# First expert's first layer for all 128 tokens, ahead of the routing result, with the tokens picked afterwards by the placement matrix

## The reference, cut to what matters

```python
x = x + gnn(layernorm(x), edge_index, W1, ..., W2, ...)          # x: (128, 768)
z = layernorm(x)
probs = softmax(z @ Wg + bg)                                      # Wg: (768, 8)
top_p = max(probs); comb = one_hot(argmax(probs)) * top_p
h = gelu(einsum('bnd,edh->ebnh', z, W1) + b1)                     # W1: (8, 768, 3072)
y = einsum('ebnh,ehd->ebnd', h, W2) + b2                          # W2: (8, 3072, 768)
ffn_out = einsum('ebnd,bne->bnd', y, comb)
scores = sigmoid(z @ Wm + bm)                                     # threshold: 12th largest score
x = x + ffn_out + small correction from ffn_out @ Wv, scores and Wo
```

## Time and profile before

| what | value |
|---|---|
| median of 3 runs | 503.6 us (502.79 to 503.71) |
| the profiled execution | 506.07 us, of which the span of the trace is 504.3 us |
| TensorE busy, matmuls | 466.4 us (92%), 2310 instructions |
| VectorE, ScalarE, GpSimd busy | 137.0, 60.6 and 33.9 us |
| read from HBM | 189.62 MB, mean 377 GB/s |
| end of the graph phase (`used` = 32) | about 151.7 us |
| first `up(0)` of the first expert | 164.85 us |
| end of the first expert's round | about 202.5 us |

### The profile page before, as it was taken

How to read it: one execution, slowest core, us unless ns; L and a number is a source line. 1 busy time by engine, 2 the same in 40 slices (tenths; PEclk the granted TensorE clock), 3 DMA queues, 4 the chain that set the end, 5 groups by cost and what they waited for, 6 DMA issues and landing times.

```text
span 504.3 us, 6062 instructions
## 1 busy us (share of the span) xinstructions
PE 466.4 (92%) x2310; PEld 232.4 (46%) x2310; DVE 137.0 (27%) x362; ACT 60.6 (12%) x113; POOL 33.9 (7%) x52
## 2 busy tenths in 40 slices
PE   7999998999999999999999999998898889789892
PEld 5656665667558344344344353352243224224352
DVE  6573698426206311010010010020010002001165
ACT  1110212002003020021020020110020011002100
POOL 3262240000000000210000000000000000000000
PEclk9999999999999999999999999999999999999996
DMA  8889998898999999999999999999999999999700
GB/s 309 305 301 402 401 400 297 307 407 323 411 357 369 417 425 423 414 423 423 423 429 423 422 428 427 420 423 430 423 423 426 427 422 423 427 423 424 297 1 31
DMA packets 32541, 190.22 MB, mean 377 GB/s; under 512 B 5423, under 2 KB 5631, under 8 KB 18190
## 3 DMA queue, kind: packets, MB, share of 16 engines
q1 hardware_dynamic: 31694, 189.94, 92.6%
q0 software_dynamic: 544, 0.05, 0.1%
q10 hardware_dynamic: 288, 0.03, 0.0%
HBM read 189.62 MB, written 0.39 MB: 377 GB/s over the span
## 4 chain that ended last, share of the span: by engine, by line
PE 60%; SPq 16%; DMA 15%; DVE 5%; issue 2%; ACT 1%; POOL 0%; DVEq 0%
PE ps L1286 17%; PE ps L1259 16%; PE ps L1081 11%; SPq L337 8%; DMA chunk<-in_L_ffn_W 7%; DMA lower<-in_L_ffn_W 6%; PE ps L1041 6%; SPq L316 4%; SPq L332 3%; PE ps L1272 2%; PE ps L1069 2%; DMA slot<-in_L_gnn_W 2%; PE ps L1096 2%; PE ps L1221 2%; SPq L354 1%
## 5 line engine op out<-in xcount | busy, mean ns | idle before, releaser
L1286 PE MATMUL ps<-lower,hidden 128*64 128x384 f32 x600 | 102.9, 491 | 6.1 <-DMA lower<-in_L_ffn_W 6.1
L1259 PE MATMUL ps<-chunk,gathered 128*64 128x512 f32 x408 | 92.6, 597 | 10.0 <-DMA chunk<-in_L_ffn_W 10.0
L1286 PEld LDWEIGHTS ps<-lower,hidden 128*64 128x64 f32 x600 | 41.3, 136 | 58.3 <-issue 45.1
L1041 PE MATMUL ps<-slot,xT 128*128 128x384 f32 x192 | 64.1, 488 | 1.2 <-DMA slot<-in_L_gnn_W 1.2
L1259 PEld LDWEIGHTS ps<-chunk,gathered 128*64 128x64 f32 x408 | 27.5, 136 | 66.9 <-issue 47.6
L1081 PE MATMUL ps<-slot,eluT 128*128 128x384 f32 x168 | 55.3, 486 | 0.0
L866 DVE TENSOR_TENSOR biased<-ps,b_T 128x384 f32<-128x384 f32 x32 | 17.1, 554 | 133.5 <-PE ps L1272 133.5
L1041 PEld LDWEIGHTS ps<-slot,xT 128*128 128x128 f32 x192 | 35.6, 190 | 23.9 <-issue 1.3
L1259 PE MATMUL ps<-extra,gathered 128*64 128x512 f32 x168 | 38.9, 598 | 4.7 <-DMA extra<-in_L_ffn_W 4.6
L1081 PEld LDWEIGHTS ps<-slot,eluT 128*128 128x128 f32 x168 | 31.5, 190 | 20.7
L874 DVE TENSOR_SCALAR place_top<-slot_no,rank,small 128x128 f32<-128x128 f32 x8 | 2.8, 346 | 136.7 <-PE ps L1309 136.7
(11 more groups left out here) (288 smaller groups left out, 282.2 us busy)
## 6 DMA issues: line engine op xcount, KB each, us to landing
lower<-in_L_ffn_W SPq DMA_DIRECT2D x50, 1152.0 KB, 26.1
chunk<-in_L_ffn_W SPq DMA_DIRECT2D x34, 1536.0 KB, 22.7
slot<-in_L_gnn_W SPq DMA_DIRECT2D x31, 1152.0 KB, 12.7
extra<-in_L_ffn_W SPq DMA_DIRECT2D x14, 1536.0 KB, 27.7
lower_on<-in_L_ffn_W SPq DMA_DIRECT2D x14, 1152.0 KB, 30.9
slot<-in_L_gnn_W SPq DMA_DIRECT2D x3, 384.0 KB, 4.6
x_sb<-in_x SPq DMA_DIRECT2D x1, 384.0 KB, 3.4
out<-xc SPq DMA_DIRECT2D x1, 384.0 KB, 2.3
```

The source lines that it names most:

```text
L1041: last = T.matmul(ps[:, 2 * (h % 2) + b, 0:HB], xT[:, 3 * half + k, :], slots[n % RING][:, k, b * HB:(b + 1) * HB], start=(n % 2 == 0 and ...
L1259: last = T.matmul(ps[b * CAP:(b + 1) * CAP, s, 0:BANK], gathered[:, k, :], upper_homes[k][:, at:at + BANK], start=(k == 0), stop=(k == KT ...
L1286: last = T.matmul(ps[c * CAP:(c + 1) * CAP, 4, 0:HB], hidden[:, q, k, b, :], lower_homes[i][:, k, c * HB:(c + 1) * HB], start=(i == 0 and ...
```

## The change

The first expert's first layer no longer waits for the gate. It is computed for all 128 tokens. What VectorE and ScalarE copy out of PSUM lands in chunk 5's own memory, scaled by the reciprocal of the standard deviation, and `first_turn` multiplies that by `place_now`: one product both picks the expert's tokens and turns the result. The gate, the ranks and the scores stand between the six `first_up`. The mean is taken out of `x1` itself, ahead of its transposes; it comes from a one-column matmul over row sums. The initial gather, the centring of the gate's weights and the `stay_warm` groups 5 to 8 are gone. SyncE's program is the same; the sixth count of `used` in the first round now comes from the first matmul of `down(0)`. The diff, cut to its core:

```diff
@@ ScalarE
-            S.copy(blocks(h2_sb[:, :]), ps[:, 0:2, 0:HB]).then_inc(h2_ready, 1)
+            S.activation(blocks(h2_sb[:, :]), ps[:, 0:2, 0:HB], ACT.Identity, accum_out=col(HSUM)).then_inc(h2_ready, 1)
...
+            act.wait_ge(mean2_ready, 1)
+            S.activation(x1[:, HB:D], x1[:, HB:D], ACT.Identity, bias=col(MEAN)).then_inc(base_half, 1)
             act.wait_ge(xT_done, 3)
-            S.copy(xT[:, 0:3, :].rearrange("p k t -> p (k t)"), ps[:, 5, 0:HB]).then_inc(xT_first, 1)
-            act.wait_ge(mean2_ready, 1)
-            S.activation(xc[:, :], x1[:, :], ACT.Square, bias=col(MEAN), accum_out=col(SS)).then_inc(squares, 1)
+            S.copy(xT[:, 0, :], ps[:, 5, 0:P]).then_inc(xT_first, 1)
+            act.wait_ge(xT_done, 4)
+            S.copy(xT[:, 1:3, :].rearrange("p k t -> p (k t)"), ps[:, 7, P:HB]).then_inc(xT_second, 1)
+            act.wait_ge(x1_part, 3)
+            S.activation(xc[:, :], x1[:, :], ACT.Square, accum_out=col(SS)).then_inc(squares, 1)
...
+                if first:
+                    for s in range(3):
+                        act.wait_ge(up_done, s + 1)
+                        S.activation(chunks[CHUNKS - 1][:, s * BANK:(s + 1) * BANK], ps[:, s, 0:BANK], ACT.Identity,
+                                     scale=col(RSTD)).then_inc(upper_ready, 1)
+                    gelu(0)
+                    gelu(1)
+                    turn_place()
+                    gelu(2)
+                    gelu(3)
+                    return
@@ VectorE
-            centre_gate()
             dve.wait_ge(att_ready, 3)
-            for b in range(2):
-                dve.wait_ge(out2_done, b + 1)
-                V.scalar_tensor_tensor(out=x1[:, b * HB:(b + 1) * HB], in0=ps[:, 2 + b, 0:HB], scalar=col(RS),
-                                       in1=x1[:, b * HB:(b + 1) * HB], op0=ALU.mult, op1=ALU.add,
-                                       accum_out=sums2[:, b:b + 1]).then_inc(x1_half, 1)
...
+            step(V.tensor_scalar(col(SHARE), col(RS), -1.0 / D, None, ALU.mult))
+            dve.wait_ge(out2_sum, 1)
+            dve.wait_ge(base_ready, 1)
+            V.tensor_scalar(col(MEAN), ps[:, 7, 0:1], col(SHARE), col(BASE), ALU.mult,
+                            ALU.add).then_inc(mean2_ready, 1)
             dve.wait_ge(mean2_ready, 1)
+            step(V.tensor_scalar(x1[:, 0:HB], x1[:, 0:HB], col(MEAN), None, ALU.add))
+            for first, end in ((0, P), (P, HB), (HB, D)):
+                half = first // HB
+                dve.wait_ge(out2_done, half + 1)
+                if half:
+                    dve.wait_ge(base_half, 1)
+                V.scalar_tensor_tensor(out=x1[:, first:end], in0=ps[:, 2 + half, first - HB * half:end - HB * half],
+                                       scalar=col(RS), in1=x1[:, first:end], op0=ALU.mult,
+                                       op1=ALU.add).then_inc(x1_part, 1)
...
-            for half in range(2):
-                dve.wait_ge(gather_done if half else gather_half, 1)
...
+                if first:
+                    for s in range(3):
+                        dve.wait_ge(wide_done, s + 1)
+                        V.tensor_scalar(chunks[CHUNKS - 1][:, WIDE + s * BANK:WIDE + (s + 1) * BANK],
+                                        ps[:, 3 + s, 0:BANK], col(RSTD), None, ALU.mult).then_inc(wide_ready, 1)
+                    add_bias(0)
+                    add_bias(1)
+                    dve.wait_ge(turned, QU)
+                    next_place()
+                    add_bias(2)
+                    take_gathered(1, 5)
+                    take_threshold()
+                    add_bias(3)
+                    return
@@ TensorE
+            T.matmul(ps[:, 7, 0:1], att_T[:, 0, :], col(HSUM), start=True, stop=True).then_inc(out2_sum, 1)
...
+            def first_up(k):
+
+                pe.wait_ge(lead_in[k], 16)
+                for bank in (0, 3, 1, 4, 2, 5):
+                    last = T.matmul(ps[:, bank, 0:BANK], xT[:, k, :], chunks[k][:, bank * BANK:(bank + 1) * BANK],
+                                    start=(k == 0), stop=(k == KT - 1))
+                    if k == KT - 1:
+                        last.then_inc(up_done if bank < 3 else wide_done, 1)
+                if k < KT - 1:
+                    last.then_inc(used, 1)
+
+            def first_turn(q):
+
+                pe.wait_ge(upper_ready, min(q + 1, 3))
+                pe.wait_ge(wide_ready, min(q + 1, 3))
                 for k in range(3):
-                    c = (3 * half + k) * P
-                    last = T.matmul(ps[:, 3 if half else 5, k * CAP:(k + 1) * CAP], xn[:, c:c + P],
-                                    place_now[:, :], start=True, stop=True)
-                last.then_inc(gather_done if half else gather_half, 1)
-            pe.wait_ge(score_ready, 1)
-            T.matmul(ps[0:1, 4, 0:P], col(SCORE), ident[:, :], start=True, stop=True).then_inc(score_turned, 1)
+                    for b in range(2):
+                        c = b * WIDE + q * HB
+                        last = T.matmul(ps[:, q, k * P + b * CAP:k * P + (b + 1) * CAP],
+                                        chunks[CHUNKS - 1][:, c + k:c + HB:3], place_now[:, :], start=True, stop=True)
+                last.then_inc(turned, 1)
...
+                                if first and i == 0 and k == 0 and c == 0:
+                                    last.then_inc(used, 1)
```

More of the change, by code:

```diff
@@ L1184, in _ @@
                      stop=True).then_inc(att_scores, 1)
[L1185 to L1188, removed]
             stay_warm(WARM[3])
@@ L1196, in _ @@
                          start=True, stop=True).then_inc(out2_done, 1)
[L1197 to L1214, removed]
-            T.matmul(ps[:, 6, 0:EXPERTS], ones[:, :], hot, start=True, stop=True).then_inc(rank_done, 1)
-            stay_warm(WARM[8], 0)
+            pe.wait_ge(mean2_ready, 1)
+            for i, (first, end, bank, at) in enumerate(((0, P, 5, 0), (P, HB, 7, P), (HB, D, 6, 0))):
+                pe.wait_ge(x1_part, i + 1)
+                for c in range(first, end, P):
+                    last = T.transpose(ps[:, bank, at + c - first:at + c - first + P], x1[:, c:c + P], ident[:, :])
+                last.then_inc(xT_done, 1)
             def gather(bank):
@@ L1243, in round_ @@
             def round_(r, first=False):
-                upper_homes, lower_homes = (chunks, lowers) if first else (chunks_on, lowers_on)
+                lower_homes = lowers if first else lowers_on
                 def landed(i):
@@ L1288, in down @@
                                                 start=(i == 0 and k == 0), stop=(i == DOWN - 1 and k == 2))
+                                if first and i == 0 and k == 0 and c == 0:
+                                    last.then_inc(used, 1)
                         last.then_inc(used, 1)
                 if first:
[L1292 to L1301 removed]
+                    pe.wait_ge(xT_first, 3)
@@ new lines, in round_ @@
+                    first_up(0)
+                    pe.wait_ge(xT_second, 1)
+                    pe.wait_ge(xT_third, 1)
+                    for k in range(KT):
+                        last = T.matmul(ps[:, 7, 0:EXPERTS + 1], xT[:, k, :], gate_w[:, k, :], start=(k == 0),
+                                        stop=(k == KT - 1))
+                    last.then_inc(logit_done, 1)
+                    first_up(1)
+                    pe.wait_ge(onehot_ready, 1)
+                    T.matmul(ps[:, 7, 16:24], later[:, :], hot, start=True, stop=True).then_inc(rank_done, 1)
@@ new lines, in round_ @@
+                    T.matmul(ps[:, 6, 0:EXPERTS], ones[:, :], hot, start=True, stop=True).then_inc(rank_done, 1)
+                    first_up(2)
+                    pe.wait_ge(score_ready, 1)
+                    T.matmul(ps[0:1, 7, P:2 * P], col(SCORE), ident[:, :], start=True,
+                             stop=True).then_inc(score_turned, 1)
+                    pe.wait_ge(top_ready, 1)
+                    T.matmul(ps[0:EXPERTS, 6, 0:P], hot_top[:, :], ident[:, :], start=True,
+                             stop=True).then_inc(hot_turned, 1)
@@ new lines, in round_ @@
+                    first_up(3)
+                    pe.wait_ge(thr_ready, 1)
+                    first_ffn()
+                    first_up(4)
+                    first_up(5)
+                    pe.wait_ge(place_ready, 1)
+                    for q in range(QU):
+                        first_turn(q)
+                    T.transpose(ps[:, 5, HB:512], place_top[:, :], ident[:, :]).then_inc(place_turned, 1)
+                    down(0)
+                    down(1)
+                    T.matmul(ps[:, 3, HB:HB + 1], ones[0:1, :], top16[0:1, KEEP - 1:KEEP], start=True,
+                             stop=True).then_inc(thr_done, 1)
@@ L1302, in round_ @@
+                    pe.wait_ge(xn_ready, 1)
+                    pe.wait_ge(place_ready, 2)
+                    pe.wait_ge(place_T_ready, 1)
+                    gather(5)
```

(13 more changed lines are left out.)

81 lines of the change are left out of this document (31 added, 50 removed).

## The result

The changed kernel takes 523.84 us (median of 4 runs, 523.41 to 524.13), where the kernel before takes 503.2 (4 runs). The ratio is 1.039, with a 95% interval of 1.0355 to 1.0426: 17.9 to 21.4 us slower. I had forecast 515.1 us and a range of 510 to 519. The direction and what bounds the kernel stand; the size does not, and the range did not hold it.

What follows compares the result with a forecast made beforehand. The load stream's last landing was taken to bound the kernel. Load 7 landing 11.0 us later plus 0.5 us at the third expert's loads gave 11.5 us, added to the median: 515.1 us, range 510 to 519.

Steps and rivals of the forecast that it cites:

- What bounds it: Expert phase: loads stream at about 424 GB/s, the last landing sets the end, 25.4 us of fixed tail follow.
- (b): To the kernel's end: TensorE stays the late one, its whole 14.4 us delay comes out, 518.0 us; 7%.
- (a): Load stream after 205 us: the queue runs faster and makes up a part, 507 to 512 us; 11%.
- (d): Second expert's loads 6 and 7: covered after all if 128-column matmuls run at 64-column pace, 503.6 us; 5%.
- TensorE's path up to the picking: First expert: first layer starts at 158.85, six products take 30.96 us, gate, ranks, scores and first_ffn together 3.97.
- The picking: Between first layer and down(0): 48 instructions at the gather's 107 ns each, 5.16 us.
- the far end: Picking products: 7.1 us if the stride of 3 costs 148 ns each, as in the strided transposes.
- The clock: Before 158.85 us: stays at 1.00 through short gaps; at 1.2 GHz a first_up would take 10.3 us instead of 5.16.
- The queue's behaviour when nearly dry: Second expert's loads: load 7 lands 5.1 to 5.5 us after issue; another 0.5 us is lost at the third expert's.
- From the profile to the median: Whole kernel: profiled execution 517.6 us, 2.5 above the median; the 11.5 us added to the median gives 515.1.
- rival (c): Picking: strided products cost 148 ns each, 1.9 us more, 517.0 us; counted inside the main case's range.
- main case: Whole kernel: 512.5 to 517.5 us around 515.1, with the last landing 11.5 us later; 73%.

Runs made afterwards that it cites:

- the two experiments: Changed kernel with twice as many moving columns in each picking product, 520.9 us; changed kernel with picking weights from consecutive columns, 518.63 us.
- the last experiment: Changed kernel with the first expert's first layer for 64 tokens alone and picking weights from consecutive columns: 504.0 us, ratio 0.9997.

## Why the prediction was off

**What bounds it: right.** The last landing sets the end, before and after; the tail is constant to 0.1 us; TensorE's time is free where the queue is full (18.6 us added, no change) and an early start gains nothing (504.0). The rival that TensorE stays the late one to the end (b) is out: the chain of the changed kernel ends in the queue as before. The rival of a made-up part (a) is out: every slice from 235 us to the last but one of the stream is at 418 to 427 GB/s. (Single windows of 4 us do pass the 430 that I took as the most, in the kernel before up to 439 GB/s at 164 us; no slice does.) The rival "not slower" (d) named its own condition, a first layer at the 64-column pace; with that and the cheap picking the time is 504.0.

**TensorE's path up to the picking: right to 0.2 us,** start (158.69 for 158.85), six products of 5.15 to 5.3 us, and what stands between them.

The miss is 523.8 - 515.1 = 8.7 us. It has three parts: load 7 landed 4.4 us later than forecast, 1.4 us more were lost behind it, and 2.9 us lie in how I carried the sum over to the median.

**The picking: the step that failed.** "I take the gather's, as form and column count are the same, and keep 7.1 as the far end." It took 8.74 us. The float32 weight load with a stride of 12 bytes costs 8.31 / 48 = 173 ns an instruction (as much with 64 moving columns as with 128, see above) where the same load from consecutive columns costs 110. My far end came from transposes, which have the stride but one instruction for each instead of two; they were the wrong row. Price of the stride, from the two experiments: 520.9 - 518.6 = 2.3 us.

**The clock: wrong place.** I looked for a fall in the gap before the first layer, and the text had only that. There it stayed at 1.00 in the changed kernel (in the last experiment's profile it was at 0.5 from 156.2 to 159.6 us, without harm to the time). It fell at the end of the picking, 6 us after TensorE had gone over from 512-column products to 64-column ones, and came back about 7 us later, 4 us into `down(0)`. Price: 523.8 - 520.9 = 2.9 us, of which the two last landings show 496.25 - 493.7 = 2.5.

Both together make load 7 go out at 204.45 instead of 199.85: 3.6 us of picking, 0.1 of the place transpose, 0.9 for the first matmul of `down(0)` at half clock. Its landing moved by 15.3 us instead of 11.0.

**The queue's behaviour when nearly dry: missed.** I let load 5 land at 188.6 and load 6 at 193.9; they landed at 190.5 and 196.6, which did not matter for load 7. I took 5.1 us for what a load needs, from one into an idle queue, and 0.5 us for what comes after load 7. The loads behind it lose more: from load 7 to the third expert's second chunk 27.2 us pass between landings, where it was 25.6 in the first profile of before and 24.1 in the one with idle matmuls in the later rounds. To the last landing it is 286.7 us, where the first profile has 284.75 and the forecast 285.3. So between the two profiled executions everything is placed: 15.3 us at load 7 and 2.0 behind it are the 17.3 by which the last landing moved.

**From the profile to the median: not sound.** My sum gave 517.6 us for a profiled execution. I took off the 2.5 us by which the profile of before lay above its median, as if every execution lost the same. The changed kernel gave nothing of this back: its four times lie between 523.4 and 524.1, its profile 0.4 below the median, while that of before lay 2.9 above. With those, 17.3 + 2.9 + 0.4 are the 20.6 us measured. Part of the 2.9 can be seen: the kernel with idle matmuls in the later rounds has the first round of the kernel before, and its last load lands at 477.3 instead of 478.95. In the first profile load 10 lands 4.3 us behind load 9, in that one 2.9. Why the changed kernel has no execution that is faster by as much is not shown.

What rival (c) called a slow picking is what happened; it stood in the main case's range with 1.9 us, and neither its clock nor the losses behind it were in the sum.

## What to carry to other kernels

Where a load queue sets the end, ask of a change only when it frees each buffer, and compare that with the landing of the load before; engine time that frees nothing late is free, and engine time saved is worth nothing. The loss begins before the queue is dry: a load that went out 1 to 2 us before the one ahead of it landed came 2.9 us late here on average, and losses of over 1 us all but ended with a lead of 8 us. So a load's time into an idle queue (5.1 us) is no measure of how early it has to go out. When the price of an instruction is taken from a row of the same form, check operand stride and the number of instructions too, and look in the trace for what TensorE's granted clock does behind a long run of 64-column products. And work out whether every execution would lose the same before adding a difference of one profile to a median.

## What the runs showed of the hardware that I had not expected

- A float32 weight load of 128 x 128, twice for each product: 110 ns from one instruction to the next from consecutive columns, 173 ns from every third one (5.30 and 8.31 us for 48, both at full clock; the second with 128 moving columns, and the changed kernel has 174 ns with 64). The transposes with that stride had 148 ns.
- The granted clock fell to 0.50 at 199.9 us although TensorE had been busy without a pause since 158.7: what it did before was six microseconds of 64-column products with weight loads between them. With 128 columns in the same products it stayed at 1.00. In the kernel with the first layer for 64 tokens it fell at 184.0, within the picking too.
- A load that was issued 1.6 us before the one ahead of it landed came 2.8 us late, and the DMA share stayed at 0.90 to 0.96 meanwhile; GB/s (329 to 359) shows it. Loads 5 and 6 of the changed kernel, with leads of 1.5 and 1.7 us, came 3.3 us late each.
